# Sums of carried values, a few edges at a time, with the products in VectorE's PSUM bank

## The reference

```python
h = jnp.maximum(_layernorm(x, axis=-1), 0.0)
x = x + _L0_gnn_ref(h, edge_index, ...)      # attention over a node's edges
h = jnp.maximum(_layernorm(x, axis=-1), 0.0)
x = x + _L1_gnn_ref(h, ..., edge_index)      # two mean-of-neighbours convolutions
h = jnp.maximum(_layernorm(x, axis=-1), 0.0)
x = x + _L2_gnn_ref(h, ..., edge_index)      # both directions of an edge
h = jnp.maximum(_layernorm(x, axis=-1), 0.0)
x = x + _L3_gnn_ref(h, ..., src, dst, edge_type_86)   # relations
```

## Time and profile before

| what | value |
|---|---|
| median of the runs | 4690.81 us |
| the profiled execution, its own time | 4694.78 us |
| its span, first to last instruction | 4693.0 us |
| GpSimd busy | 3469.0 us, 74% |
| VectorE busy | 2870.1 us, 61% |
| TensorE matmul busy | 2328.5 us, 50% |
| ScalarE busy | 958.4 us, 20% |

### The profile page before, as it was taken

How to read it: one execution, slowest core, us unless ns; L and a number is a source line. 1 busy time by engine, 2 the same in 40 slices (tenths; PEclk the granted TensorE clock), 3 DMA queues, 4 the chain that set the end, 5 groups by cost and what they waited for, 6 DMA issues and landing times. The chain is left out here.

```text
span 4693.0 us, 30595 instructions
## 1 busy us (share of the span) xinstructions
PE 2328.5 (50%) x8870; PEld 1409.5 (30%) x8870; DVE 2870.1 (61%) x3600; ACT 958.4 (20%) x1485; POOL 3469.0 (74%) x3151
## 2 busy tenths in 40 slices
PE   7820067775777730000622331177764677666562
PEld 3410034443555420000622331022221444443331
DVE  8866177775888756666311110166665899988783
ACT  0012022221445421111000000144442111111110
POOL 7777677774777747776588888777774777777777
PEclk9865555555989875555655555588886787877776
DMA  1035244441444432222122222344442111110100
GB/s 29 12 95 166 47 95 100 98 98 59 151 151 156 147 110 66 65 71 66 6 5 5 5 5 5 56 156 151 151 151 81 29 29 29 32 28 26 28 26 9
DMA packets 348969, 327.82 MB, mean 70 GB/s; under 512 B 223275, under 2 KB 295862, under 8 KB 347596
## 3 DMA queue, kind: packets, MB, share of 16 engines
q1 hardware_dynamic: 85600, 236.67, 14.0%
q0 software_dynamic: 144256, 45.62, 10.1%
q10 hardware_dynamic: 118944, 43.56, 3.9%
HBM read 170.38 MB, written 156.58 MB: 70 GB/s over the span
## 5 line engine op out<-in xcount | busy, mean ns | idle before, releaser
L1378 POOL DMA_INDIRECT sum_table<-e_add_rows,e_add_idx x392 | 612.7, 1563 | 142.4 <-issue 118.0
L536 POOL DMA_INDIRECT g_ring<-x_table,pos x392 | 412.3, 1052 | 173.7 <-issue 119.2
L536 POOL DMA_INDIRECT c_ring<-x_table,pos x392 | 398.9, 1018 | 175.8 <-issue 131.0
L1919 PE MATMUL g_pX<-w,g_h_T 128*128 128x512 f32 x784 | 438.2, 709 | 177.8 <-DVEq L1776 177.5
L536 POOL DMA_INDIRECT f_ring<-con_table,pos x392 | 419.3, 1070 | 134.5 <-issue 127.6
L1739 POOL DMA_INDIRECT out_x<-g_out_rows,end_index x392 | 426.7, 1088 | 119.5 <-issue 119.5
L536 POOL DMA_INDIRECT d_ring<-g_table,pos x392 | 389.4, 993 | 167.2 <-issue 124.0
L536 POOL DMA_INDIRECT b_ring<-h_table,src x392 | 405.9, 1035 | 132.9 <-issue 126.0
L345 POOL DMA_INDIRECT x_dst<-in_x,dst x392 | 400.3, 1021 | 134.2 <-issue 134.2
L1648 PE MATMUL f_pH<-f_T,w2in 128*128 128x448 f32 x672 | 319.8, 622 | 274.4 <-DVE f_T L1540 274.4
L1429 PE MATMUL e_pS<-e_values,e_equal 128*128 128x18 f32 x784 | 169.0, 378 | 379.8 <-DVEq L1403 379.8
(11 more groups left out here) (346 smaller groups left out, 5033.2 us busy)
## 6 DMA issues: line engine op xcount, KB each, us to landing
f_sums<-sum_table ACTq DMA_DIRECT2D x126, 238.0 KB
sum_table<-c_zero SPq DMA_DIRECT2D x39, 715.0 KB, 5.3
g_table<-c_g SPq DMA_DIRECT2D x42, 448.0 KB, 2.5
h_table<-a_xp SPq DMA_DIRECT2D x28, 560.0 KB, 3.7
a_x<-in_x SPq DMA_DIRECT2D x28, 448.0 KB, 5.9
b_h_node<-h_table ACTq DMA_DIRECT2D x28, 448.0 KB, 4.4
b_x_node<-in_x SPq DMA_DIRECT2D x28, 448.0 KB, 4.9
x_table<-b_x_node SPq DMA_DIRECT2D x28, 448.0 KB, 2.5
```

The costliest lines, as they stand in the source:

```text
L536: pool.indirect_dma_start(out=ring[:, t, :], out_offset=None, in_=table, in_offset=bass.IndirectOffsetOnAxis(ap=idx[:, c * C + t:c * C + t ...
L1378: pool.indirect_dma_start(out=g.sums[b], out_offset=bass.IndirectOffsetOnAxis(ap=aidx[:, c % 2, t:t + 1], axis=0), in_=add[:, c % 2, t, :] ...
L1919: last = nc.tensor.matmul(pX[d % 2][:, j * 512:(j + 1) * 512], tsb[:, 0, quad], g.w3[:, (2 * d + j) % 4, :], start=True, stop=True)
```

## The change

A new function, `add_in_bank`, takes the place of `sum_with_carry` in stages c, d and g, and of `sum_back` in stage g. The product goes into a spare part of `w.bank` instead of the output tile, and the sum reads it from there. The spare part has 340 values in stage c, 344 in d and 292 in g, which is room for 10, 10 and 9 edges of 32 features; so a chunk is done in pieces of 10, 10 and 8 edges in c and d, and of four times 7 edges in g. In `finish` the sum also stays in the bank, and the step of L1812 is done piece by piece from there. Stages e and f keep the old functions.

```diff
+def add_in_bank(nc, dve, bank, car, by, more, out, last=None):
+    K = car.shape[1]
+    most = bank.shape[1] // K
+    n = -(-C // -(-C // most))
+    for lo in range(0, C, n):
+        ts = slice(lo, min(C, lo + n))
+        width = ts.stop - lo
+        area = bank[:, 0:width * K].rearrange("p (t f) -> p t f", f=K)
+        nc.vector.tensor_tensor(area, bc_tile(car, width), bc_feat(by[:, ts], K), ALU.mult)
+        dve.drain()
+        nc.vector.tensor_tensor(area if last else out[:, ts], area, more[:, ts], ALU.add)
+        dve.drain()
+        if last:
+            last(out[:, ts], area, ts)
+            dve.drain()
...
 def stage_sage_first(nc, g):
+        spare = w.bank[:, Norm.USED + F + C:512]
-                sum_with_carry(nc, dve, g, cr.pc, run[:], c, mean[:])
+                add_in_bank(nc, dve, spare, cr.pc, g.pre[:, part(c)], swap(run[:]), mean[:])
...
 def stage_sage_second(nc, g, late):
+        spare = w.bank[:, Norm.USED + 2 * C:512]
-                sum_with_carry(nc, dve, g, cr.pc, run[:], c, mean[:])
+                add_in_bank(nc, dve, spare, cr.pc, g.pre[:, part(c)], swap(run[:]), mean[:])
...
 def stage_relations(nc, g):
+        spare = w.bank[:, 192 + C:512]
...
             def x_full(c):
                 nc.vector.tensor_copy(after, g.x_in[:, c, :])
                 dve.drain()
-                sum_back(nc, dve, g, after, g.by_feature(c), c, xf[:])
-                dve.drain()
+                add_in_bank(nc, dve, spare, after, g.suf[:, part(c)], swap(g.by_feature(c)), xf[:])
...
             def finish(c):
-                sum_with_carry(nc, dve, g, cr.pc, run[:], c, out[:, a])
-                nc.vector.scalar_tensor_tensor(out=out[:, a], in0=out[:, a], scalar=0.0, in1=swap(g.by_feature(c)), op0=ALU.max,
-                                               op1=ALU.add)
+                def positive_plus_x(to, area, ts):
+                    nc.vector.scalar_tensor_tensor(out=to, in0=area, scalar=0.0, in1=swap(g.by_feature(c))[:, ts], op0=ALU.max,
+                                                   op1=ALU.add)
+                add_in_bank(nc, dve, spare, cr.pc, g.pre[:, part(c)], swap(run[:]), out[:, a], last=positive_plus_x)
                 dve.drain().then_inc(out_ready, 1)
```

## The result

The changed kernel takes **4633.68 us** (median of four runs, 4631.4 to 4634.52) against 4690.86 us; the ratio is 0.9879 with an interval from 0.9863 to 0.9895. The profiled execution took 4634.52 us with a span of 4632.8. The spans, 4693.0 and 4632.8 us, lie 60.2 us apart and the medians 57.2: the profiled execution of before took 3.9 us more than its median, that of after 0.8, so some 3 of the 60.2 us belong to the two executions and not to the change.

A forecast was written before the change was run, and what follows sets the result against it. GpSimd's indirect DMAs, held by VectorE sums with two SBUF inputs, were taken to bound stages c, d and g; gains of 10 + 12 + 35 = 57 us off 4690.8 gave 4634 us, range 4620 to 4664.

The forecast's parts named there:

- What holds GpSimd: Stages c, d, g: VectorE sums with two SBUF inputs lengthen indirect DMAs; freeing them gives 63.6 us at most.
- the inference of the Trainium skill: Rule set against the forecast: `tensor_tensor` doesn't stall GpSimd's DMAs, so nothing is gained; some 4693 us.
- The rival that the change doesn't do what it says: Sums with one PSUM input still hold GpSimd, 37 us instead of 63.6; time 4670; chance 0.04.
- scans and products that stay: Stages c, d, g: cause given for the lengthening of GpSimd's instructions beyond 13.1, 14.4 and 36.1 us.
- VectorE's additions: Smaller pieces cost VectorE +0.9 us a chunk in c and d, +3.3 in g, its turn there 69.0 us.
- both rivals in which VectorE's price decides: Stage g: dearer PSUM operands, 4640 to 4672, chance 0.16; or slower, as at 4708, chance 0.07.
- the 21.8 us of slack would be spent just so: End of stage g: VectorE and GpSimd arrive together, at 4609 and 4610, so g gains 35 us.
- each further us a chunk costs about 13: Stage g: every further us per chunk on VectorE costs about 13 us.
- 6.5 for the two together: Stage d: L1278 and scan L1191 hold gathers after the change, 0 to 1.09 us a chunk; 6.5 us charged.
- the term that was mis-sized: Stage c's gain: 13.1 us freed, less 0.9 and 2, makes 10 us.
- The tail behind the last gather was charged 2.9 us: Stage c: VectorE's last chunk takes 0.9 us more and comes about 2 us later against the shorter gathers.
- next to nothing but the 0.30 us: Stages c and d: GpSimd's only notable wait is 0.30 us between indirect DMAs, 391 times.

The follow-up runs named there:

- e8_whole_psum: Kernel before, whole sums of 896 values in c, d and g with the carried row in PSUM as first input, marked product left out: 4621.28 us, ratio 0.9873.
- e3_pieces_sbuf: Changed kernel with the same pieces in an SBUF tile instead of the PSUM bank, in c, d and g: 4641.64 us, ratio 0.992.
- e4_after_more_dve: Changed kernel with five fills of 292 values on VectorE added in each chunk of stage g: 4664.82 us, ratio 0.9944.
- e5_before_more_dve: Kernel before with five fills of 292 values on VectorE added in each chunk of stage g: 4698.33 us, ratio 1.0003.
- e7_g_three: Changed kernel with 32 more values of the bank freed, so stage g takes three pieces instead of four: 4632.71 us, ratio 0.9879.
- e12_changed: The changed kernel again, no edit, on another chip: 4631.36 us, ratio 0.988.
- e1_cd: Kernel before with the change in stages c and d alone: 4660.2 us, ratio 0.9955.
- e2_g: Kernel before with the change in stage g alone: 4655.59 us, ratio 0.9947.
- e11_before_d_x: Kernel before with stage d's scaled mean added to x from the bank, piece by piece: 4693.44 us, ratio 1.0008.
- e6_d_x: Changed kernel with stage d's scaling and addition to x also done from the bank, piece by piece: 4627.17 us, ratio 0.9857.

## Why the prediction was right, and which terms were off

The time, 4633.68 against 4634, hits closer than its terms, and that is luck: c was 7.3 us too small, d and g together 4.4 too large, and the 3 us left over are what the two profiled executions differ from their medians by.

**What holds GpSimd** was right: two SBUF inputs on VectorE, not the length and not the read across the layout. The forecast rested on one row for the last point; `e8_whole_psum` and `e3_pieces_sbuf` now show both sides. They also decide about the inference of the Trainium skill, SBUF — State Buffer, section "Who interferes with whom", by which a `tensor_tensor` would not stop what GpSimd's DMAs need: for these indirect DMAs the trace disagrees (0.94 us with a PSUM input, 1.38 with two in SBUF, under sums of the same 320 values). The same section says besides that a VectorE instruction with two SBUF inputs contends with a GpSimd instruction that reads SBUF; the trace agrees with that if an indirect DMA, which takes its list of rows from an SBUF tile (`pos`), counts as one. The prediction set only the inference against its rows. The rival that the change doesn't do what it says is out.

Two SBUF inputs are not the only hold, though. The prediction gives the rest of the excess to "scans and products that stay"; part of it in stage g is neither. L1787 (L1766 before) is a `tensor_scalar` with one tensor input, the edge types in SBUF. In the kernel after, timeline of stage g, VectorE and GpSimd:

```profile
4167.75 1.09 DVE L1811 TENSOR_TENSOR g_rel<-g_rel,norm_bank 128x896 f32<-128x896 f32 x1
4168.53 1.62 POOL L536 DMA_INDIRECT g_ring<-x_table,pos  x1 [0.30 <-issue]
4168.75 1.28 DVE L1787 TENSOR_SCALAR g_etype<-g_etype,relid 86x2048 f32<-86x2048 int32 x1
```

The gather begins under an instruction with one input in PSUM, which by rows 5 and 6 should let it go, but ends 0.12 us behind the end of L1787, which began 0.22 us after it. Of the 27 gathers and scatters that were running when an L1787 began, 26 end 0.12 or 0.13 us behind its end (25 of 26 in the kernel before, with L1766). The change leaves this as it is; no run removed it.

**VectorE's additions** were right: 0.400, 0.564 and 0.555 us, 69.2 us a turn. Instructions that write to the bank and read from it carry no surcharge beyond 0.014 us over the estimate, so that both rivals in which VectorE's price decides are out. The estimate of 0.065 us for each from the Trainium skill, VectorE: DVE Perf Modes, section "The TRN2 errata", finds nothing in the rows: a whole sum takes 1.80 us with its first input in PSUM (`e8_whole_psum`) and 1.82 with both in SBUF.

**Stage g**: the step that the 21.8 us of slack would be spent just so came out to 0.9 us, with GpSimd waiting 1.95 us for VectorE, and the gain to 33.2 us instead of 35. `e4_after_more_dve`, `e5_before_more_dve` and `e7_g_three` show that it is a tie. The sentence that each further us a chunk costs about 13 was right too: stage g grew by 34.9 us for 2.6 us a chunk, 13.4 for each.

**Stage d**: L1299 holds 12 gathers for 7.4 us, and the scan 3 for 1.0; the prediction had 6.5 for the two together. The tail behind the last gather grew by 1.4 us instead of 0.9 (56.7 against 55.3), and 19.2 - 8.4 - 1.4 is the 9.4 us measured (8.9 in `e12_changed`, 12.1 in `e1_cd`).

**Stage c is the term that was mis-sized**, 17.3 against 10. What was held under L849, 13.1 us, is gone as predicted; c's scan holds 2.3 us more than before (17.8 against 15.5), by its phase. Two things were wrong in the sum. The tail behind the last gather was charged 2.9 us and grew by only 0.4 (43.6 against 43.2 us). And GpSimd's own idle time within the stage fell by 6.7 us, which the prediction had read as fixed ("next to nothing but the 0.30 us"). 13.1 - 2.3 - 0.4 + 6.7 = 17.1, of the 17.3 us.

That idle time is three long gaps, behind the 113th, the 225th and the 337th gather. The first of them in the kernel before, timeline of stage c with SyncE's queue:

```profile
1267.40 1.08 DVE L954 TENSOR_TENSOR c_x_node<-c_x_node,c_pG 128x896 f32<-128x896 f32 x1
...
1268.50 0.32 SPq L916 DMA_DIRECT2D x_table<-c_x_node  x1
1268.87 2.30 SPq L929 DMA_DIRECT2D sum_table<-c_zero  x3
...
1269.64 0.94 POOL L536 DMA_INDIRECT c_ring<-x_table,pos  x1 [0.30 <-issue]
...
1273.05 1.09 DVE L136 TENSOR_REDUCE norm_bank<-c_ring 128x28 f32<-128x896 f32 x1 [4.57 <-DMA c_ring<-x_table,pos]
...
1274.83 0.94 POOL L536 DMA_INDIRECT c_ring<-x_table,pos  x1 [4.25 <-issue]
```

and the second of them in the kernel after, VectorE, GpSimd and SyncE's queue:

```profile
1407.86 0.94 POOL L536 DMA_INDIRECT c_ring<-x_table,pos  x1 [0.30 <-issue]
1408.59 0.32 SPq L936 DMA_DIRECT2D x_table<-c_x_node  x1
1408.95 1.55 SPq L949 DMA_DIRECT2D sum_table<-c_zero  x3
...
1409.10 0.94 POOL L536 DMA_INDIRECT c_ring<-x_table,pos  x1 [0.30 <-issue]
1410.38 1.09 DVE L136 TENSOR_REDUCE norm_bank<-c_ring 128x28 f32<-128x896 f32 x1 [1.83 <-DMA c_ring<-x_table,pos]
...
1412.16 0.94 POOL L536 DMA_INDIRECT c_ring<-x_table,pos  x1 [2.12 <-issue]
```

In both, GpSimd goes on 1.78 us behind the moment when VectorE's wait for the rows gathered so far ends (1273.05 to 1274.83, 1410.38 to 1412.16). In stage c of the fourteen traces of this case there are 42 such gaps; in 26 of them VectorE waits for those rows, and the distance is 1.78 or 1.79 us in all 26. So in these 26 the gap is as long as the rows take to land. They seem to land late in the kernel before because L954, ended at 1268.48, lets SyncE issue a store of 448 KB at 1268.50, 2.1 us before the gap, and right behind it three writes of 715 KB (`sum_table<-c_zero`); some 400 GB/s are moved from 1270.5 to 1273 (16 GB/s from 1266 to 1268). In the second fence the same burst is issued, but its store 1.45 us before the gap, and the rows land 2.1 us sooner. VectorE's loop hangs on the gathers, so this burst met all three gaps at the same distance, 4.25 us each. In the kernel after, the gaps are 1.94, 2.12 and 1.97 us. It is not quite the holds of L849 alone: in `e1_cd`, which has none in stage c, the third gap still met its store, 2.75 us before the gap, with 4.35 us, and in `e2_g` and `e5_before_more_dve`, whose stage c is as before, one of the three is short (1.86 and 2.85 us). That is read from the traces; no run moved the store or the writes alone, so it is argued and not shown by experiment.

## What to carry to other kernels

Where GpSimd's indirect DMAs set the pace, look for VectorE instructions with both inputs in SBUF and give one input a place in PSUM, even if that takes more and smaller instructions on VectorE: the rows show at once which are in the way, since a held DMA ends a fixed time behind the VectorE instruction (0.82 or 0.83 us behind these sums, 0.75 behind the scans of c and d, 0.12 behind L1787, which has one SBUF input and holds all the same). Before that, measure the slack of the engine that takes the extra work, to the end of the stage, because the gain ends where that slack does. And count anew what escapes by phase: a pair that costs nothing now can cost the moment another hold is taken away.

## What had not been expected of the hardware

- GpSimd paused in stages b, c, d and f after every 112 gathers (never in g, where scatters lie between them): in c until the rows gathered so far had landed, and 1.78 us more wherever that could be measured, so 1.9 to 2.1 us in the kernel after, and 4.25 before, where a burst of writes had begun 2.1 us ahead of the gap.
- A sum with two SBUF inputs did not hold an indirect DMA that was already running: in the kernel before, L849, L1447 and L1278 began 0.03 to 0.93 us behind the start of 72 gathers and scatters and lengthened none, while in the kernel after a gather that began 0.39 us behind L1299's start was held until 0.82 us behind its end. L1787 was another matter: in the kernel after it held 13 that had begun up to 0.34 us before it, and let go the one that had begun 0.57 us before it.
- An edit can be worth nothing in one kernel and some 6 us in the next, as the phases would have it (`e11_before_d_x` and `e6_d_x`).
